# Mean squares of the queries' remainder and of the keys in two halves of TensorE's rows, and both inverses ahead of the first residual

## The reference

```python
q = rmsnorm(x @ w_qa, q_norm_w) @ w_qb          # 192 latent columns, 16 heads
kv = x @ w_kva                                  # 64 latent columns and 64 of the rotary key
kv_c, k_rope = (kv[..., :KV_LORA], kv[..., KV_LORA:])
kv = rmsnorm(kv_c, kv_norm_w) @ w_kvb
...
scores = jnp.einsum('blhd,bmhd->bhlm', q, k) * scale   # causal softmax, values
return out.reshape(B, L, H * DV) @ w_o
```

## Time and profile before

| | us |
|---|---|
| median of 3 runs | 1368.81 |
| the three runs | 1367.03, 1368.81, 1376.04 |
| span of the profiled execution, first to last instruction | 1372.1 |
| TensorE busy in it | 1236.2 |
| VectorE busy | 801.9 |
| ScalarE busy | 463.7 |
| GpSimd busy | 376.6 |

### The profile page before, as it was taken

The page is one execution under the profiler, slowest core; times in us unless marked ns, Lnnn a source line. Parts: engine busy times, 40 slices in busy tenths (PEclk is TensorE's granted clock), DMA queues, the critical chain, the costliest instruction groups (busy, mean ns, idle before and its releaser), DMA issues.

```text
span 1372.1 us, 19483 instructions
## 1 busy us (share of the span) xinstructions
PE 1236.2 (90%) x6005; PEld 767.3 (56%) x6005; DVE 801.9 (58%) x2226; ACT 463.7 (34%) x1057; POOL 376.6 (27%) x464
## 2 busy tenths in 40 slices
PE   6999999989999899988959999997585987999988
PEld 3566566555555466556536777775244545555454
DVE  6377767786578667784513434334665673685431
ACT  2455435442455335442201111111331612625310
POOL 1242023451425413351340000113564261311200
PEclk9799999999999999999979999999777998999999
DMA  9999999999800100010336888884212021000000
GB/s 320 413 419 420 420 421 420 420 420 418 334 1 32 62 1 1 8 58 30 107 103 191 274 263 269 270 278 138 67 43 62 1 70 39 12 12 16 0 16 16
DMA packets 89422, 235.48 MB, mean 172 GB/s; under 512 B 12768, under 2 KB 23680, under 8 KB 89088
## 3 DMA queue, kind: packets, MB, share of 16 engines
q1 hardware_dynamic: 70912, 192.54, 37.9%
q0 software_dynamic: 9216, 25.18, 5.8%
q10 hardware_dynamic: 9216, 16.78, 3.2%
HBM read 66.70 MB, written 167.77 MB: 171 GB/s over the span
## 4 chain that ended last, share of the span: by engine, by line
PE 72%; DVE 15%; issue 4%; another core or an unknown queue 3%; ACT 2%; SPq 2%; DMA 1%; POOL 1%; ACTq 0%; DVEq 0%; POOLq 0%
PE bank L521 6%; PE bank L547 5%; PE bank L480 4%; PE bank L609 4%; PE bank L530 4%; PE bank L481 4%; PE bank L1327 4%; PE bank L1349 3%; PE bank L1588 3%; PE bank L1594 3%; DVE negmax L853 3%; PE bank L1605 3%; DVE r L864 2%; PE bank L1639 2%
## 5 line engine op out<-in xcount | busy, mean ns | idle before, releaser
L700 ACT ACTIVATE r<-bank,negmax 128x128 f32<-128x128 f32 (+3 forms) x256 | 134.9, 527 | 173.7 <-DVE negmax L853 163.5
L521 PE MATMUL bank<-r 128*128 128x512 f32 (+3 forms) x512 | 184.2, 443 | 0.0
L853 DVE TENSOR_REDUCE negmax<-bank 128x1 f32<-128x128 f32 (+3 forms) x256 | 124.1, 485 | 55.9 <-PE bank L522 53.0
L530 PE MATMUL bank<-tables,r 128*128 128x128 f32 x640 | 117.7, 284 | 19.8 <-DVE r L864 18.6
L964 POOL TENSOR_TENSOR r<-r,tables 128x256 f32<-128x256 f32 x56 | 42.0, 749 | 331.7 <-ACT r L681 331.6
L1198 POOL DMA_INDIRECT sent<-r,slots x96 | 93.9, 978 | 113.0 <-ACT r L700 49.1
L530 PEld LDWEIGHTS bank<-tables,r 128*128 128x128 f32 x640 | 75.2, 145 | 74.6 <-issue 35.6
L1436 DVE COPY r<-bank 128x512 f32<-128x512 f32 x64 | 41.2, 685 | 116.3 <-PE bank L1358 75.3
L864 DVE TENSOR_SCALAR r<-r,rrow 128x128 f32<-128x128 f32 (+3 forms) x256 | 103.8, 406 | 0.3
L521 PEld LDWEIGHTS bank<-r 128*128 128x128 f32 x512 | 77.8, 191 | 23.6 <-issue 18.4
L1214 POOL DMA_INDIRECT r<-sent,slots x16 | 15.2, 950 | 223.3 <-DMA sent<-r 219.6
(11 more groups left out here) (276 smaller groups left out, 2404.4 us busy)
## 6 DMA issues: line engine op xcount, KB each, us to landing
sent<-gath SPq DMA_DIRECT2D x8, 16384.0 KB, 88.1
r<-waT_dram SPq DMA_DIRECT2D x64, 304.0 KB, 3.1
r<-sent SPq DMA_DIRECT2D x64, 256.0 KB
sent<-r ACTq DMA_DIRECT2D x64, 256.0 KB
w2buf<-wcT_dram SPq DMA_DIRECT2D x64, 48.0 KB, 3.5
r<-w_o_dram SPq DMA_DIRECT2D x1, 2048.0 KB, 11.2
sent<-gath SPq DMA_DIRECT2D x2, 1024.0 KB, 56.7
out_dram<-x SPq DMA_DIRECT2D x4, 512.0 KB, 2.9
```

What stands on the lines that cost most here:

```text
L521: nc.tensor.matmul(at[:, 0:n], QT[g % 2][:, h, i * P:(i + 1) * P], KT[:, 0:n], start=True, stop=False)
L530: last = nc.tensor.transpose(bank[TRANS[u % 2]][:, j * P:(j + 1) * P], prob[:, u % 4, j * P:(j + 1) * P], ident)
L700: nc.scalar.activation(prob[:, u % 4, 0:(i + 1) * P], bank[SCORE[u % 4]][:, 0:(i + 1) * P], ACT.Exp, bias=negmax[:, u:u + 1], scale=1.0, a ...
L853: nc.vector.tensor_reduce(negmax[:, u:u + 1], bank[SCORE[u % 4]][:, 0:(i + 1) * P], axis=AX.X, op=ALU.max, negate=True).then_inc(A["max"], 1)
```

## The change

The array `sq` has two slices instead of three: the squares of the keys go to partitions 64 to 127 of the slice whose partitions 0 to 63 hold the remainder of the queries. `mean_squares(b)` is one piece for both: the matmul over 128 partitions as before, and then, for each half of the columns, one matmul over partitions 0 to 63 into bank 3 and one over partitions 64 to 127 into bank 7. Both results are there at the same time, so VectorE takes both inverses one after the other: in the front ahead of `rope_keys(0)`, in the row change ahead of `residual(b, 0)`. Bank 7 brings two waits in the front: `mean_squares(0)` waits until the transposes of row 2 are evacuated (`row_v` at 3), and `prep_queries`, which writes bank 7, until the keys' sum has been read (`inv` at 3).

```diff
--- before.py
+++ after.py
@@ -163,7 +163,7 @@
         KT, e = carve(r2, e, (SEQ,))
         V, e = carve(r2, e, (TB, KVL))
         prob, e = carve(r2, e, (4, SEQ))
-        sq, e = carve(r2, e, (3, SEQ))
+        sq, e = carve(r2, e, (2, SEQ))
         rq, e = carve(r2, e, (SEQ,))
         rk, e = carve(r2, e, (SEQ,))
         krope, e = carve(r2, e, (2, SEQ))
@@ -371,6 +371,7 @@
             loaded(pe, "prep")
             pe.wait_ge(N0[0].done["row"], BATCH + 1)
             pe.wait_ge(N0[0].done["row_v"], BATCH - 1)
+            pe.wait_ge(A["inv"], 3)
             for h in range(HEADS):
                 c = (h % 8) * KVL
                 nc.tensor.matmul(bank[4 + h // 8][:, c:c + KVL], wqbT[:, h, 0:P], wkvT[:, 0, h, :],
@@ -453,17 +454,19 @@
                                                 xnT[:, k, row_tokens(b)], start=(k == 0), stop=(k == KC - 1))
                     last.then_inc(A["proj"], 1)
 
-            def mean_squares(b, n):
-
-                if n == 0:
-                    pe.wait_ge(A["sq"], 3 * b + 3)
-                    nc.tensor.matmul(bank[3][:], ones[:], sq[:, 0, :], start=True, stop=False)
-                    nc.tensor.matmul(bank[3][:], ones[0:QL2, :], sq[0:QL2, 1, :], start=False, stop=True)\
-                        .then_inc(A["ms"], 1)
-                else:
-                    pe.wait_ge(A["inv"], 4 * b + 1)
-                    nc.tensor.matmul(bank[3][:], ones[0:KVL, :], sq[0:KVL, 2, :], start=True, stop=True)\
-                        .then_inc(A["ms"], 1)
+            def mean_squares(b):
+
+                pe.wait_ge(A["sq"], 3 * b + 3)
+                if b == 0:
+                    pe.wait_ge(N0[0].done["row_v"], BATCH - 1)
+                nc.tensor.matmul(bank[3][:], ones[:], sq[:, 0, :], start=True, stop=False)
+                for c in range(0, SEQ, 2 * P):
+                    last_q = nc.tensor.matmul(bank[3][:, c:c + 2 * P], ones[0:QL2, :], sq[0:QL2, 1, c:c + 2 * P],
+                                              start=False, stop=c + 2 * P == SEQ)
+                    last_kv = nc.tensor.matmul(bank[7][:, c:c + 2 * P], ones[QL2:P, :], sq[QL2:P, 1, c:c + 2 * P],
+                                               start=True, stop=True)
+                last_q.then_inc(A["ms"], 1)
+                last_kv.then_inc(A["ms"], 1)
 
             def row_values(b):
 
@@ -618,12 +621,11 @@
             for b in (1, 2):
                 for k in range(KC):
                     norm_tensor(pe, N0[b], b, xn[:, TB * b:TB * (b + 1), :], k)
-            mean_squares(0, 0)
+            mean_squares(0)
             pe.wait_ge(N0[0].done["row"], 2)
             pe.wait_ge(N0[0].done["row_v"], 2)
             for k in range(KC):
                 norm_tensor(pe, N0[3], 3, xn[:, TB * 3:, :], k)
-            mean_squares(0, 1)
             prep_queries(pe)
             row_values(0)
             loaded(pe, "tables")
@@ -643,10 +645,8 @@
                     project(b + 1)
                 slot(b * GROUPS + GROUPS - 1, NU + 4, False)
                 if more:
-                    mean_squares(b + 1, 0)
+                    mean_squares(b + 1)
                 output(b, 0)
-                if more:
-                    mean_squares(b + 1, 1)
                 output(b, 1)
                 output(b, 2)
                 if more:
@@ -659,9 +659,10 @@
         def att_scalar(act):
             def squares(b):
 
-                for m, n, width in ((0, P, QL), (1, QL2, QL), (2, KVL, KVL)):
+                for m, n, to, width in ((0, P, sq[:, 0, :], QL), (1, QL2, sq[0:QL2, 1, :], QL),
+                                        (2, KVL, sq[QL2:P, 1, :], KVL)):
                     act.wait_ge(A["proj"], 3 * b + m + 1)
-                    nc.scalar.activation(sq[0:n, m, :], bank[m][0:n, :], ACT.Square,
+                    nc.scalar.activation(to, bank[m][0:n, :], ACT.Square,
                                          scale=1.0 / math.sqrt(width)).then_inc(A["sq"], 1)
 
             def root(b, n):
@@ -778,7 +779,7 @@
 
                 r = rq if n == 0 else rk[0:KVL, :]
                 dve.wait_ge(A["ms"], 2 * b + n + 1)
-                nc.vector.tensor_scalar(r, bank[3][:] if n == 0 else bank[3][0:KVL, :], RMS_EPS, None, ALU.add)\
+                nc.vector.tensor_scalar(r, bank[3][:] if n == 0 else bank[7][0:KVL, :], RMS_EPS, None, ALU.add)\
                     .then_inc(A["inv"], 1)
                 dve.wait_ge(A["inv"], 4 * b + 2 * n + 1)
                 nc.vector.reciprocal(r, r).then_inc(A["inv"], 1)
@@ -921,10 +922,10 @@
             norm_evacuate(dve, nc.vector.tensor_copy, N0[1], 1, 1, row="row_v")
             norm_evacuate(dve, nc.vector.tensor_copy, N0[2], 2, 1, row="row_v")
             inverse(0, 0)
+            inverse(0, 1)
             loaded(dve, "tables")
             rope_keys(0)
             latents(0, 0)
-            inverse(0, 1)
             latents(0, 1)
             first_ropes(0)
             for b in range(BATCH):
@@ -933,9 +934,9 @@
                 if more:
                     rope_keys(b + 1)
                     inverse(b + 1, 0)
+                    inverse(b + 1, 1)
                 residual(b, 0)
                 if more:
-                    inverse(b + 1, 1)
                     latents(b + 1, 0)
                 stats_of(b, 0)
                 residual(b, 1)
```

## The result

| | before | changed |
|---|---|---|
| median, three runs of before (six: 1368.70), six of the change | 1368.81 us | 1378.11 us |
| ratio, the same chip, six runs each | | 1.0070, 95% interval 1.0045 to 1.0095 |
| ratio, measured again later (E7) | | 1.0049, 1.0026 to 1.0071 |
| span of the profiled execution | 1372.1 us | 1376.9 us |

The change makes the kernel slower by 0.5 to 0.7%, that is 7 to 10 us (with the intervals 4 to 13), where +8.5 us and 1377 us were forecast.

A forecast was written before the change was run, and what follows sets the result against it. TensorE, busy 90% of the span, was taken as the bound. Front +7.4 us and three row changes +1.1 us sum to +8.5 us; with the median of 1368.8 us the forecast was 1377 us, range 1369 to 1385.

The forecast's parts named there:

- What bounds: Whole kernel: TensorE, busy 90% of the span; time counts on its stream or on what that stream waits for.
- The keys' own matmul, 1.05 us for each place: Front and three row changes: removing the keys' 512-column matmul over 64 rows shortens TensorE by 1.05 us each.
- Row change, +0.37 each: Three row changes: output tile 2 waits 1.6 us for the late residual, so each loses 0.37 us, +1.1 in all.
- The pairs at no cost: Mean squares: four 256-column matmuls in two row halves run at once, 0 us added; the other bound was 0.86.
- The rival of row halves in turn: Mean squares: halves run one after another, TensorE +0.86 us per place, +10.2 in all, 1379 us; chance 0.15.
- The front, +4.3 us by the wait for `inv` 3: Front: `prep_queries` waits for the second inverse and starts at 31.6 instead of 27.29 us; TensorE idles 3.8 us.
- The front, +3.1 us by the clock: Front: after the idle gap all 16 heads run slowly at 1.03 us, making the front +7.4 instead of +4.3 us.
- The clock behind the front, set to nothing, 2 us either way: First query products: slow for the same length as before until the clock rises; may differ 2 us either way.
- The pause in the row change bringing the clock down: Rival, three row changes: the 1.6 us wait before output tile 2 halves the clock; +18.7 us, 1387; chance 0.06.
- The term that was too large: Row change, VectorE: the second inverse's reciprocal starts 0.73 us after that inverse starts.
- The delay reaches the end whole: After attention: no later row waits for a fixed time, so all +8.5 us reach the end.

The follow-up runs named there:

- E7: The change again with no edit, against the kernel before: ratio 1.0049 (1.0026 to 1.0071), first product at 50.60 us.
- E1: The change with its front undone (mean squares of row 0 apart, both new waits gone), against the kernel before: ratio 1.0023 (1.0001 to 1.0044).
- E2: The change's front with the old row changes, against the kernel before: ratio 1.0046 (1.0022 to 1.0071).
- E4: The change with the `inv` 3 wait moved to the ninth head of `prep_queries`, against the kernel before: ratio 1.0019 (0.9997 to 1.0042).
- E3: The change with four unread 512-column matmuls in the front's pause, against the kernel before: ratio 1.0029 (1.0005 to 1.0053).
- E6: The change with one 512-column matmul per row half instead of two of 256; single run without ratio, attention's end at 654.4 us.
- E5: Old front; row changes read both sums first, first residual between the reciprocals; against the kernel before: ratio 0.9958 (0.9936 to 0.9980).

## Why the prediction was right, point by point

- *What bounds.* TensorE's stream: right. Every shift of the first product was still there at attention's end to within 1.4 us in the change, E1, E2, E4 and E7; E3's first product was 4.6 us late and its attention's end 5.1, E6's 6.8 and 5.1.
- *The keys' own matmul, 1.05 us for each place.* Right that it is saved, shown by E5; the size is 1.25 in the row changes. The forecast counted from L465's start on and left out the 0.2 us ahead of it. The 0.37 did not suffer by it, since they come from the times at which tile 2 starts (1.6 less 1.25, not less 1.05). The pairs at no cost: right (1.07 us for four in two halves). The rival of row halves in turn is out, by the rows of the change and by E6. The Trainium skill, "TensorEngine Tiling (Array Packing)", section "Key Properties", says that tiles run independently, and here they do (starts 0.01 us apart).
- *The front, +4.3 us by the wait for `inv` 3.* Right: the first head at 31.81, forecast 31.6; 4.5 us late. E4 takes 2.8 of them away by moving this wait alone; the other 1.7 are the later mean squares behind the wait for `row_v`, which the forecast had in its sum too (25.32 to 26.9).
- *The front, +3.1 us by the clock.* Right: all 16 heads at 1.03 us; E3 gives 2.9 of it back by filling the pause. The rule of the Trainium skill that spoke against the change, from "TensorE: Matmul & The Clock Gate", section "Why this matters for your kernels", held: behind 3.8 us without work the heads took 1.03 us. It is no sharp edge here: in E6 the clock fell late enough that L475 came at 47.49 instead of 48.2 to 48.4, in E3 it was still up at 36.
- *The clock behind the front, set to nothing, 2 us either way.* It gave 1.3 us back in this profile: the first product was 7.49 us late and the next output tile 0 only 6.15 (178.72 for 172.57). In E7 it gave 0.5 (7.65 and 7.15). Within the 2 us.
- *Row change, +0.37 each.* Right in sign and place; the size is 0.28. The term that was too large is the second addition ahead of its reciprocal: I took 0.73 from start to start, it took 0.65 (182.82 to 183.47), 0.08 of the 0.09.
- *The pause in the row change bringing the clock down* (the slower rival): did not happen; the stretches around it are at 1.00. The range was said to take this rival in, but its price, 1387, lay outside 1369 to 1385. A closer row than the one it named was there: the stretch from 311.8 to 315.2 of before had 1.15 us of work, and the next one was at 0.50.
- *The delay reaches the end whole.* Right within what can be seen: 6.8 and 7.1 us at attention's end in the two profiles, 7 to 10 in the ratios, and the unchanged rest varies by more than the difference. That the median came within 1.1 us of the 1377 is in part luck for the same reason; the positions in the front and in the row changes are what the mechanism is shown by.

## What to carry to other kernels

A matmul that shares the array with another saves its time only if the engine that reads both results does not put a second long operation in front of something that TensorE waits for. When two results come at once, put what TensorE waits for between the long operations and not behind them (E5, which also empties both banks first), and put a wait for a bank at the first instruction that writes this bank, not ahead of the loop (E4). A pause on TensorE ahead of small matmuls has to be counted twice, once as a wait and once in the clock of what follows.

## What the runs showed of the hardware

- Two matmuls of 64 rows in different row halves of the array and into different banks start 0.01 us apart and take the time of one, at 256 and at 512 columns (1.07 and 1.06 us to the next instruction).
- The granted clock fell while TensorE idled, between 28 and 31.5 us in the change; four matmuls without a use in this pause kept it up (E3), and then it fell later, among the small matmuls, between 34 and 39 us. In before it fell among them too, with TensorE busy throughout (0.50 from 32 us on).
- Once down, the clock stayed down through all that was left of the small matmuls in each of the runs, and came back among the query products behind them: before at 0.50 until 48.8 us and at 1.00 from 50 on, with the first product at 42.95; the change at 1.00 from 54 on, with it at 50.44.
- A matmul over 64 rows between matmuls over 128 rows cost 1.25 us of TensorE's time in the row change of before, 0.2 ahead of it and 1.05 from its start, where as many columns over 128 rows take 0.86 (a quarter of a tile's 3.45).
